# A gated delta-rule layer on one core: the inverse's third stage moved behind the projection and the old state, its first join spread over four column groups

## The reference

```python
q = short_conv(x @ Wq)                  # 8 heads of 128, 4 taps, silu, l2 norm
k = short_conv(x @ Wk); v = short_conv(x @ Wv)   # 3 keys and 3 values per token and head
beta = 2 * sigmoid(x @ Wb); g = -exp(A_log) * softplus(x @ Wa + dt_bias)
def step(S, (qt, kt, vt, bt, gt)):      # S is 128 x 128 for each head
    S = S * exp(gt)
    for i in range(3):
        S = S + bt[i] * outer(kt[i], vt[i] - kt[i] @ S)
    return S, qt @ S
out = (rmsnorm(o) * silu(x @ Wg)) @ Wo
```

## Time and profile before

| | |
|---|---|
| median of 3 runs | 8200.72 us (8177.36 to 8208.36) |
| profiled execution, its own time | 8192.18 us |
| its span | 8190.3 us |
| mean granted clock | 0.943 |
| PE busy | 7430.0 us, 91% |
| DVE busy | 6462.9 us, 79% |
| ACT busy | 5489.7 us, 67% |
| POOL busy | 4121.4 us, 50% |

### The profile page before, as it was taken

One profiled execution on the slowest core, in us unless ns is written; L12 is line 12 of the kernel. 1 busy time (PEld: TensorE's weight loads), 2 busy tenths in 40 slices (PEclk: granted clock), 3 DMA queues, 4 the chain that ended last, 5 costly groups with the idle time before them and its releaser, 6 DMA issues. The chain is left out here.

```text
span 8190.3 us, 425307 instructions
## 1 busy us (share of the span) xinstructions
PE 7430.0 (91%) x155940; PEld 6299.3 (77%) x155940; DVE 6462.9 (79%) x22300; ACT 5489.7 (67%) x20343; POOL 4121.4 (50%) x6333
## 2 busy tenths in 40 slices
PE   5999999989999998989999999899898999889999
PEld 3788787878787777878787778787777777767777
DVE  4888888888888888888888888888888888623333
ACT  3777777777777777777777777777777777533333
POOL 0555555555555555555555555555555555511111
PEclk6899999999999999999999999999999999889999
DMA  2000000000000000000000000000000000010000
GB/s 90 8 9 9 10 9 9 9 9 9 9 10 10 9 9 10 10 9 10 9 9 10 9 10 9 9 9 9 10 10 10 9 10 10 7 32 8 10 8 8
DMA packets 283513, 96.57 MB, mean 12 GB/s; under 512 B 226096, under 2 KB 276544, under 8 KB 281152
## 3 DMA queue, kind: packets, MB, share of 16 engines
q1 hardware_dynamic: 281408, 68.93, 3.8%
HBM read 52.08 MB, written 16.78 MB: 8 GB/s over the span
## 5 line engine op out<-in xcount | busy, mean ns | idle before, releaser
L821 DVE SCALAR_TENSOR_TENSOR CY<-PP,CWV,CY 128x128 f32<-128x128 f32 x4608 | 1587.8, 345 | 141.2 <-ACT CY L738 54.3
L821 DVE SCALAR_TENSOR_TENSOR CY<-PP,CWK,CY 128x128 f32<-128x128 f32 x4608 | 1585.0, 344 | 99.0 <-ACT CY L738 27.0
L1033 POOL TENSOR_TENSOR UM<-U,C 32x256 f32<-32x256 f32 x1536 | 1107.3, 721 | 119.6 <-POOL UM L1033 24.2
L1026 POOL TENSOR_TENSOR Y<-U,C 32x256 f32<-32x256 f32 x768 | 555.2, 723 | 1136.7 <-DVE UQ L914 1096.6
L552 PE MATMUL PI<-T,WB 32*32 32x32 f32 x49152 | 749.8, 195 | 312.0 <-DVE T L830 309.3
L552 PEld LDWEIGHTS PI<-T,WB 32*32 32x32 f32 x49152 | 638.0, 110 | 477.0 <-issue 411.7
L532 PE MATMUL PP<-XT,WK 128*128 128x131 f32 x3072 | 789.7, 342 | 80.1 <-DVE CY L821 79.9
L532 PE MATMUL PP<-XT,WV 128*128 128x131 f32 x3072 | 740.2, 324 | 126.7 <-DVE CY L821 82.6
L738 ACT ACTIVATE CY<-PP,CWK 128x128 f32<-128x128 f32 x1536 | 567.1, 369 | 399.0 <-PE PP L532 389.4
L1006 POOL TENSOR_TENSOR S<-R,BETA 96x4 f32<-96x4 f32 x512 | 102.0, 199 | 1341.2 <-DVE R L874 1341.2
L1239 ACT ACTIVATE HS<-PH,B1S 128x512 f32<-128x512 f32 x512 | 352.5, 689 | 608.0 <-PE PH L1158 608.0
(11 more groups left out here) (228 smaller groups left out, 18937.6 us busy)
## 6 DMA issues: line engine op xcount, KB each, us to landing
EX<-exd SPq DMA_DIRECT2D x768, 32.0 KB
exd<-EXS SPq DMA_DIRECT2D x16, 512.0 KB, 2.7
XR<-in_L_attn_x SPq DMA_DIRECT2D x65, 64.0 KB, 2.7
XL<-in_L_attn_x SPq DMA_DIRECT2D x16, 256.0 KB, 2.9
XRES<-in_L_attn_x SPq DMA_DIRECT2D x64, 64.0 KB, 2.6
x<-X SPq DMA_DIRECT2D x64, 64.0 KB, 1.6
XI<-x SPq DMA_DIRECT2D x16, 256.0 KB, 2.8
out<-OUT SPq DMA_DIRECT2D x16, 256.0 KB, 2.3
```

The costliest lines, as they stand in the source:

```text
L821: dve.scalar_tensor_tensor(CY[:, m % RING], ptile(m)[:, s:s + P], taps_of(m)[:, s:s + 1], CY[:, m % RING], ALU.mult, ALU.add).then_inc(tap ...
L1026: pool.tensor_tensor(Y1[r, :, :], U[r, par, :, r], over(first[r, :], [BK, NHEAD, BK], 1), ALU.mult).then_inc(seed_sb, 1)
L1033: pool.tensor_tensor(UM[r, lv], U[r, par, :, r], over(merge[lv][r, :], [BK, NHEAD, BK], 1), ALU.mult).then_inc(made, 1)
```

## The change

Two edits. In slot 4, PE does `project` and `old_state` first and the inverse's third stage (stage 2) behind them, ahead of join 2. And the matmuls of join 1 write four groups of 32 PSUM partitions instead of two: those of the middle block of even heads partitions 32 to 63, of odd heads 0 to 31, those of the lower block of even heads 64 to 95, of odd heads 96 to 127. ACT gathers them with four copies instead of two.

```diff
+        mids = PB[:, 0:4 * BK].rearrange("p (q c) -> p q c", q=4)
+        his = PB[:, 0:8 * BK].rearrange("p (q c) -> p q c", q=4)
...
                     for k in range(SLOTS):
-                        if do_inv and k in INV_AT:
+                        if do_inv and k in INV_AT and k != 4:
                             invert(invn, 1 - par, INV_AT[k])
                         if known(i, 0, NSC):
                             project(i, half, SLOTS * c + k)
                         if k in (1, 4) and do_run:
                             old_state(k // 4, run, rs, rc)
+                        if do_inv and k == 4:
+                            invert(invn, 1 - par, INV_AT[k])
...
                             for h in range(NHEAD):
-                                pe.matmul(join[mid, h, 0:BK], U[:, par, h, mid], X3[:, h, 0:BK], start=True, stop=True)
-                                mm = pe.matmul(join[hi, h], U[:, par, h, hi], X3[:, h], start=True, stop=True)
+                                q, o = h // 2, 1 - h % 2
+                                pe.matmul(mids[CT * o:CT * o + CT, q], U[:, par, h, mid], X3[:, h, 0:BK], start=True, stop=True)
+                                o = 2 + h % 2
+                                mm = pe.matmul(his[CT * o:CT * o + CT, q], U[:, par, h, hi], X3[:, h], start=True, stop=True)
...
-                            act.activation(GA[BK:2 * BK, :, 0:BK], join[BK:2 * BK, :, 0:BK], ACT.Copy, scale=-1.0)
-                            act.activation(GA[2 * BK:R], join[2 * BK:R], ACT.Copy, scale=-1.0).then_inc(join_sb, 1)
+                            for e in range(2):
+                                o = CT * (1 - e)
+                                act.activation(GA[BK:2 * BK, e:NHEAD:2, 0:BK], mids[o:o + CT], ACT.Copy, scale=-1.0)
+                                o = CT * (2 + e)
+                                op = act.activation(GA[2 * BK:R, e:NHEAD:2], his[o:o + CT], ACT.Copy, scale=-1.0)
+                            op.then_inc(join_sb, 1)
```

## The result

The changed kernel takes 8383.99 us (median of 4 runs, 8371.74 to 8419.82), the kernel before 8202.78 us beside it: a ratio of 1.0235, with a 95% interval of 1.0203 to 1.0267. It is slower, as forecast, but by 181 us where 55 were forecast.

What follows compares the result with a forecast made beforehand. It took PE and DVE together to bound slots 3 to 7, plus half clock. Chain +1.35, clock -1.15, new fall +0.8 made +1.0 us per super-step, 64 us on 8192.18: 8256 us, range 8215 to 8300 (eight in ten: 8130 to 8385).

Steps and rivals of the forecast that it cites:

- What bounds the kernel: PE and DVE together bound slots 3 to 7, meeting at slot 7; half clock costs 3.6 us per super-step.
- Join 1 on PE: Join 1 takes 0.58 us instead of 1.02, 0.44 less per chunk; counted as 0 at full clock, lengthening PE's wait.
- The copies: ACT's four copies of join 1 take 1.29 us per chunk, 0.32 us more; costed at nothing in c = 1 to 3.
- the late silu: In c = 0, the silu behind the copies, awaited by slot 3's key transposes, comes 0.32 us later.
- Slot 4, the chain: Later third stage delays DVE; by slot 7, c = 0 to 3 lose 0.5, 0.05, 0.4, 0.4: 1.35 us per super-step.
- The clock: Falls in c = 2 stay at 0.95 per super-step, gaining 1.15 us; a possible new fall in c = 0 costs 0.8.
- I give it a third: Chance that the clock falls behind the new 1.5 us wait for the silu in c = 0; priced at 0.8 us.
- 1.0 us of slack: PE's idle time before slot 7 in c = 0, subtracted from the 3.4 us price of a new fall there.
- more falls: Rival: new falls behind waits in c = 0 (always) and c = 3 (half the time); 8435 us, half 8320; chance 0.2.
- the clock is kept: Rival: the shorter c = 2 wait ends falls; 8072 us with all gone, 8130 with six in ten; chance 0.24.

Runs made afterwards that it cites:

- e2: Only join 1 in four column groups with its four copies, old slot 4, on the kernel before; 8609.74 us, ratio 1.0501.
- e7: Kernel before with four-group join 1, four copies, old slot 4, plus two unread matmuls behind join 1; 8193.79 us, ratio 1.0020.
- e3b: Changed kernel with unread matmuls ahead of PE's waits: slot 3 in c = 0, and slots 4, 5 and 7; 8087.94 us, ratio 0.9904.
- e4b: Kernel before with unread matmuls ahead of slot 3 in c = 0 and the third stage in c = 1 to 3; 7993.97 us, ratio 0.9790.
- e8: Changed kernel with five unread matmuls ahead of the key transposes of slot 3 in c = 0 alone; 8169.50 us, ratio 0.9977.
- e1: Only the new slot 4 order, with join 1 and its two copies as before, on the kernel before; 8118.36 us, ratio 0.9909.
- e10: Kernel before with four unread matmuls ahead of slot 4 in c = 2 alone; 8054.72 us, ratio 0.9845.
- e9: Kernel before with slot 4 as projection, third stage, old state, and the old join 1; 8092.95 us, ratio 0.9888.

## Why the prediction was wrong

**What bounds the kernel** held: DVE and PE meet in slot 7, and half clock costs 3.6 us per super-step. With the waits filled the kernel before takes 104.38 us per super-step at full clock on average, where 104.30 had been read from a single one.

**Join 1 on PE** was right in its size (0.58 us forecast, 0.59 measured), but taken as 0 at full clock with the remark that it makes the wait longer. That longer wait was the costly part: alone it is worth 5.0%, of which 4.8 points are gone when the 0.44 us are given back (e2, e7).

**The copies** were right (1.29 us; the rows of the new copies are 268 and 376 ns), and so was the late silu.

**Slot 4, the chain** was right in kind and about twice too high in size: 0.7 us per super-step at full clock against 1.35. DVE's wait is 0.31 us in c = 1 to 3 where I took 0.4, and 0.95 us in c = 0 where I took 1.0. By chunks, e3b against e4b at full clock (medians, which sum to a little more than the difference of the means), c = 0 is 0.56 us longer (forecast 0.5), c = 1 0.01 (0.05), c = 2 0.28 (0.4) and c = 3 0.10 (0.4).

**The clock** is the step that failed, in the sentence "I give it a third" and in the falls that it left out. The sum had 0.95 falls per super-step in c = 2, a third of one in c = 0 and none elsewhere. The changed kernel has 3.4 per super-step, where the kernel before has 1.1 (0.8 of them in c = 2), and 17.8 us of half clock against 10.4. By chunks:

- c = 0 is 2.84 us longer; the sum had 0.5 + 0.8 = 1.3. The new wait came out to the hundredth (1.51 us), but the clock fell behind it in 36 of 53 super-steps and not in a third, nearly as often as behind the 2.3 us wait before (43 of 55). And I subtracted 1.0 us of slack that did not come back: PE then waits ahead of slot 7, and the clock fell there 29 times.
- c = 1 is 1.55 us longer; the sum had 0.05 and no fall. There are 34. With the wait in c = 0 filled (e8) there is none, and both chunks are nearly back at their old length.
- c = 2 is 1.17 us shorter; the sum had 0.4 - 1.15 = -0.75. It has no fewer falls, 51 for 43, but 5.8 us of half clock per chunk for 8.0.
- c = 3 is 0.43 us longer; the sum had 0.4. This agrees in part by luck, since the 17 falls there were not in it.

As an estimate, 0.7 us of chain and 0.35 x 7.4 = 2.6 us for the added half clock make 3.3 of the 3.44 us; the forecast had 1.35 for the first and -1.15 + 0.8 = -0.35 for the second. It also priced a fall at 3.4 us; the many short ones of the changed kernel come to 0.35 x 5.2 = 1.8 us each, and it is their number that makes the loss. The rival "more falls", which had the wait in c = 0 always take the clock and that in c = 3 half the time, named the mechanism but not c = 1; with its whole price it gave 8435 us, with half 8320, and the measured 8384 lies between.

**The two edits against each other.** The order alone (e1) cuts the wait in c = 2 to 1.4 us. No fall comes right behind it any more, and those that come ahead of and behind slot 7 are short: 5.5 us of half clock per super-step for 10.4. So the rival "the clock is kept" is in the main what the order alone does (0.9% faster), and the shorter join takes it back and more. My sum added the two edits; they work against each other through one wait.

**Length of the wait, and what follows it.** Falls in slots 3 to 6, by the wait ahead of them:

| wait, us | where | falls, of so many waits |
|---|---|---|
| 1.15 | before, c = 1 | 0 of 54 |
| 1.24 | before, c = 3 | 4 of 54 |
| 1.31 | e10, c = 2 | 0 of 54 |
| 1.58 | e2, c = 1 | 15 of 52 |
| 1.67 | e2, c = 3 | 24 of 51 |
| 2.31 | before, c = 2 | 43 of 55 |
| 2.68 | e2, c = 2 | 51 of 51 |

In these the third stage follows at once (in e10 the unread matmuls stand ahead of the wait). Where the projection follows, the same length gives both answers: 0 of 56 in e1 (1.45 us, then the old state), 32 of 55 in e9 (1.47 us, then 0.31 us more of waiting and the third stage). So the length alone does not decide. Left open is what else does: in c = 1 of the changed kernel and of e8 the waits are the same (0.78 and 0.62 us), and the clock falls behind them only in the first.

## What to carry to other kernels

Where PE waits regularly and its granted clock is under 1.0 behind the waits, price the waits by the clock first: compare a super-step at clock 1.00 with the mean, and count the falls place by place. Shortening PE work ahead of such a wait can then cost far more than it saves, and before an order is tuned, a few unread matmuls in the wait tell whether the order or the clock is being measured. A new fall can also bring others behind it, as c = 0 did in c = 1. An edit that splits one long wait into two may win by the clock what it loses on the chain, so the two edits of a change should be timed apart.

## What the runs showed of the hardware

Removing 0.44 us of PE work per chunk made the kernel 5.0% slower, and adding two matmuls per chunk that nobody reads took the ratio from 1.0501 back to 1.0020. Half clock costs about 0.35 us for each us of it in this kernel; a fall came to 3.4 us in the kernel before, more than the wait of 2.33 us ahead of it. With a longer wait ahead of the third stage the clock fell more often, from 0 of 54 at 1.15 us to 51 of 51 at 2.68 us. And with unread matmuls in those waits (e4b), which write only 32 partitions, the granted clock was 1.00 over whole super-steps.

One more wait is in all of these traces and was not looked into; in the kernel before, 1000 to 6900 us, it reads:

```profile
PE PP L532 <- issue: 41.0, 10, 4.8
```

These have no releaser in the profile. With three more of 2.9 to 3.0 us that it puts down to DVE's taps they are thirteen waits, one in every fourth super-step, ahead of its first projection, and half clock comes with each of them. No filled kernel is rid of them: in e4b the super-steps that hold them take 107.5 us on average against 104.4 for the rest. What PE waits for there is open.
